# Attention stage of a transformer layer: which probability tiles TensorE takes whole, which engine makes three of the low parts, and in which steps the row maxima are found

## The reference

```python
attn = jnp.einsum('bhqd,bhkd->bhqk', q, k) * SCALE
causal = jnp.tril(jnp.ones((s, s), dtype=bool))
attn = jnp.where(causal[None, None], attn, -jnp.inf)
probs = jax.nn.softmax(attn, axis=-1)
out = jnp.einsum('bhqk,bhkd->bhqd', probs, v)
```

## Time and profile before

| | before |
|---|---|
| median of 3 runs | 1719.4 us (1718.43 to 1723.72) |
| profiled execution: its own time | 1721.68 us |
| profiled execution: span | 1719.9 us |
| PE busy | 1660.3 us (97%) |
| DVE busy | 1161.7 us (68%) |
| ACT busy | 1104.9 us (64%) |
| POOL busy | 906.1 us (53%) |
| mean granted clock of PE | 0.988 |

### The profile page before, as it was taken

One profiled execution on the slowest core, in us unless ns is written; L12 is line 12 of the kernel. 1 busy time (PEld: TensorE's weight loads), 2 busy tenths in 40 slices (PEclk: granted clock), 3 DMA queues, 4 the chain that ended last, 5 costly groups with the idle time before them and its releaser, 6 DMA issues.

```text
span 1719.9 us, 30467 instructions
## 1 busy us (share of the span) xinstructions
PE 1660.3 (97%) x9262; PEld 1369.7 (80%) x9262; DVE 1161.7 (68%) x2377; ACT 1104.9 (64%) x1684; POOL 906.1 (53%) x764
## 2 busy tenths in 40 slices
PE   7999999999999999999986999999999999999996
PEld 7987677767767776776665999999999999999992
DVE  6437777777777777778697676665665566556544
ACT  3222788787878887887686566666665565556544
POOL 2321888878788888882764433434334343343422
PEclk9999999999999999999997999999999999999998
DMA  7676211111111111112664897897987887788776
GB/s 241 188 220 196 62 50 50 49 49 49 49 49 49 49 49 49 49 49 74 232 229 128 287 269 225 245 274 208 281 237 201 224 265 217 208 249 239 192 190 217
DMA packets 103715, 276.87 MB, mean 161 GB/s; under 512 B 19833, under 2 KB 37625, under 8 KB 93625
## 3 DMA queue, kind: packets, MB, share of 16 engines
q1 hardware_dynamic: 78169, 213.29, 38.0%
q0 software_dynamic: 25440, 62.27, 17.4%
HBM read 194.75 MB, written 63.72 MB: 150 GB/s over the span
## 4 chain that ended last, share of the span: by engine, by line
PE 87%; DVE 6%; issue 2%; DMA 2%; ACT 2%; POOL 1%; SPq 0%; DVEq 0%; ACTq 0%; POOLq 0%
PE p_prj L91 26%; PE a_op L883 11%; PE a_mp L842 8%; PE a_sp L901 7%; PE p_at_ps L91 7%; PE p_logit_ps L91 7%; PE e_qp L91 5%; PE a_op L874 5%; PE p_ht_ps L2057 3%; PE e_vp L91 2%; PE p_at_ps L2080 2%; DVE part_max L759 2%; PE a_sp L905 1%; PE a_shared L860 1%; PE a_mp L845 1%
## 5 line engine op out<-in xcount | busy, mean ns | idle before, releaser
L709 POOL TENSOR_TENSOR prob_lo<-prob,prob_hi 128x1024 fp32r<-128x1024 f32 x211 | 451.5, 2157 | 141.6 <-DVE prob_hi L788 132.6
L759 DVE TENSOR_REDUCE part_max<-a_mp 128x1 f32<-128x512 f32 (+2 forms) x600 | 359.5, 610 | 70.5 <-PE a_mp L842 40.4
L1446 POOL DMA_INDIRECT acc_rows<-m_y_out,m_row_ids x108 | 176.1, 1631 | 410.7 <-ACT m_y_out L1615 385.9
L744 ACT ACTIVATE prob<-a_sp 128x1024 f32<-128x1024 f32 x320 | 293.6, 930 | 64.4 <-PE a_sp L905 34.9
L91 PE MATMUL p_prj<-m_w_hi,m_ht_hi 128*128 128x352 f32 x888 | 297.5, 335 | 1.8 <-DVE m_ht_lo L1855 1.4
L91 PE MATMUL p_prj<-m_w_lo,m_ht_hi 128*128 128x352 f32 x888 | 288.0, 324 | 0.0
L91 PE MATMUL p_prj<-m_w_hi,m_ht_lo 128*128 128x352 f32 x888 | 287.0, 323 | 0.0
L1879 DVE TENSOR_TENSOR m_w_lo<-m_w_raw,m_w_hi 128x704 fp32r<-128x704 f32 (+1 forms) x357 | 270.7, 797 | 22.8 <-ACT m_w_hi L1621 22.4
L1621 ACT ACTIVATE m_w_hi<-m_w_raw 128x704 fp32r<-128x704 f32 (+1 forms) x357 | 229.0, 713 | 17.5 <-PE p_prj L91 16.8
L1865 DVE TENSOR_TENSOR m_at_lo<-p_at_ps,m_at_hi 128x384 fp32r<-128x384 f32 x111 | 61.8, 557 | 252.0 <-ACT m_at_hi L1607 252.0
L731 ACT ACTIVATE prob_hi<-prob 128x1024 fp32r<-128x1024 f32 x216 | 203.2, 941 | 6.8
(11 more groups left out here) (314 smaller groups left out, 3336.0 us busy)
## 6 DMA issues: line engine op xcount, KB each, us to landing
m_w_raw<-wexp SPq DMA_DIRECT2D x51, 1408.0 KB
m_w_raw<-wexp SPq DMA_DIRECT2D x51, 768.0 KB
qk_parts<-rows SPq DMA_DIRECT2D x64, 256.0 KB, 3.2
multi<-qk_parts SPq DMA_DIRECT2D x42, 256.0 KB, 5.0
acc_rows<-p_zeros SPq DMA_DIRECT2D x2, 4352.0 KB, 18.8
v_head<-v_all SPq DMA_DIRECT2D x16, 520.0 KB, 3.0
k_stack<-qk_parts SPq DMA_DIRECT2D x21, 256.0 KB, 4.1
q_stack<-qk_parts SPq DMA_DIRECT2D x21, 256.0 KB, 6.2
```

The source lines that it names most:

```text
L709: nc.gpsimd.tensor_tensor(prob_lo[:, t % RING, :, c0:NB], prob[:, t % RING, :, c0:NB], f32(prob_hi[:, t % RING, :, c0:NB]), ALU.subtract). ...
L744: nc.scalar.activation(prob[:, t % RING, :, c0:NB], sp_[:, t % 2, :, c0:NB], ACT.Exp, scale=SCALE).then_inc(prob_ready, 1)
L759: nc.vector.reduce_max(part_max[:, qb, kb:kb + 1], mp[:, n % 2, 0:width], AX_X).then_inc(piece_done, 1)
L1446: nc.gpsimd.indirect_dma_start(acc_dram[sum_of(t)], bass.IndirectOffsetOnAxis(ap=row_id(t), axis=0), y_out[:, t % 4, :], None, compute_op= ...
```

## The change

Four things change, all in the attention:

- In heads 0 to 14 the whole tiles are 10 and 18 in place of 7, 17 and 18. Head 15 keeps 7, 17 and 18; the new function `whole_tiles(h)` chooses.
- `LO_POOL` was all tiles but 0, 1, 10 and the whole ones: 2 to 6, 8, 9, 11 to 16 and 19, 14 tiles. It becomes all but 0, 1, 2 and the whole ones: 3 to 9, 11 to 17 and 19, 15 tiles. DVE makes the low parts of 0, 1 and 2 in place of 0, 1 and 10.
- ACT makes `prob_hi` of tiles 7 and 17 and no longer of 10.
- `PIECES_AT`, the pieces in each step of heads 1 to 14, goes for steps 5 to 19 from 3 4 3 4 2 1 2 1 3 3 3 3 3 3 2 to 3 3 3 3 3 2 3 2 3 3 3 3 2 2 2. The 24th piece then falls in step 13 instead of 14 (as the rule `first_part_done` counts, `row_maxima "a"` moves from step 15 to 14).

```diff
--- before.py
+++ after.py
@@ -529,7 +529,7 @@
 RING = 5
 
 
-PIECES_AT = (0, 0, 0, 0, 0, 3, 4, 3, 4, 2, 1, 2, 1, 3, 3, 3, 3, 3, 3, 2)
+PIECES_AT = (0, 0, 0, 0, 0, 3, 3, 3, 3, 3, 2, 3, 2, 3, 3, 3, 3, 2, 2, 2)
 PIECES_AT_FIRST = (1, 1, 1, 2, 2, 3, 3, 3, 3, 2, 1, 2, 1, 2, 2, 2, 2, 2, 3, 2)
 assert sum(PIECES_AT) == sum(PIECES_AT_FIRST) == NPC and NS == len(PIECES_AT) == len(PIECES_AT_FIRST) and NS % RING == 0
 
@@ -550,9 +550,9 @@
 FW = VW + 1
 
 
-WHOLE = {7, 17, 18}
+WHOLE, WHOLE_LAST = {10, 18}, {7, 17, 18}
 HI_DVE, HI_DVE_LAST = {2, 3, 9}, {1, 2, 3, 4, 5, 8, 9, 11, 13, 15, 19}
-LO_POOL, LO_POOL_LAST = set(range(NS)) - {0, 1, 10} - WHOLE, {0}
+LO_POOL, LO_POOL_LAST = set(range(NS)) - {0, 1, 2} - WHOLE, {0}
 
 def load_projection(sp, flat, wproj_dram, wgate_dram, landed):
 
@@ -566,6 +566,10 @@
 
 def lo_pool_tiles(h):
     return LO_POOL_LAST if isinstance(h, int) and h == H - 1 else LO_POOL
+
+
+def whole_tiles(h):
+    return WHOLE_LAST if isinstance(h, int) and h == H - 1 else WHOLE
 
 
 def count_before(which, t):
@@ -629,7 +633,7 @@
         if t in tiles:
             eng.wait_ge(hi_dve, h * len(HI_DVE) + (count_before(tiles, t) + 1))
         else:
-            eng.wait_ge(hi_act, h * (NS - len(HI_DVE | WHOLE)) + (t - count_before(tiles | WHOLE, t) + 1))
+            eng.wait_ge(hi_act, h * (NS - len(HI_DVE | WHOLE)) + (t - count_before(tiles | whole_tiles(h), t) + 1))
 
     def wait_lo(eng, h, t):
 
@@ -637,7 +641,7 @@
         if t in tiles:
             eng.wait_ge(lo_pool, h * len(LO_POOL) + (count_before(tiles, t) + 1))
         else:
-            eng.wait_ge(lo_dve, h * (NS - len(LO_POOL | WHOLE)) + (t - count_before(tiles | WHOLE, t) + 1))
+            eng.wait_ge(lo_dve, h * (NS - len(LO_POOL | WHOLE)) + (t - count_before(tiles | whole_tiles(h), t) + 1))
 
     def sync_part(sp):
         def load_head(h, p):
@@ -725,7 +729,7 @@
             nc.scalar.activation(o_sb[:, j % 2, :], op[0:VW, :], ACT.Copy).then_inc(out_copied, 1)
 
         def high_part(h, t):
-            if t not in hi_dve_tiles(h) | WHOLE:
+            if t not in hi_dve_tiles(h) | whole_tiles(h):
                 c0 = S_TILES[t][2]
                 act.wait_ge(prob_ready, h * NS + (t + 1))
                 nc.scalar.activation(prob_hi[:, t % RING, :, c0:NB], prob[:, t % RING, :, c0:NB],
@@ -788,7 +792,7 @@
                 nc.vector.tensor_copy(prob_hi[:, t % RING, :, c0:NB], prob[:, t % RING, :, c0:NB]).then_inc(hi_dve, 1)
 
         def low_part(h, t):
-            if t in lo_pool_tiles(h) | WHOLE:
+            if t in lo_pool_tiles(h) | whole_tiles(h):
                 return
             c0 = S_TILES[t][2]
             wait_hi(dve, h, t)
@@ -866,7 +870,7 @@
             j, kp, c0 = S_TILES[t]
             if parts[0] == 0 and t == J_FIRST[j] and not (isinstance(h, int) and h == 0 and j == 0):
                 pe.wait_ge(out_copied, h * NTB + j)
-            if t in WHOLE:
+            if t in whole_tiles(h):
                 if parts[0] == 0:
                     pe.wait_ge(prob_ready, h * NS + (t + 1))
                 for b in parts:
```

## The result

The changed kernel takes 1729.35 us (median of 5 runs, 1728.6 to 1730.3), the kernel before 1720.55 us (5 runs, 1718.43 to 1723.72): ratio 1.0046, 95% interval 1.0034 to 1.0058. The forecast was 1691 us and the range ended at 1707.

The account below looks back on a forecast made before the run. PE was taken as the bound, busy 40.48 of 41.00 us a head. Terms -0.87 - 1.2 + 0.1 = -1.97 us over 14 heads, with heads 0 and 15, gave -28.4: 1719.4 to 1691 us, range 1683 to 1707.

Parts of the forecast that it names:

- PE's own work: Matmuls of whole tiles in steps 1, 11 and 14: two whole tiles lost, one gained, -0.87 us a head.
- The cast of tile 9 under POOL's tiles: DVE's cast now meets a busy POOL: 0.5 us for DVE, 0.1 for PE with late low parts, ends 0 and 1.5.
- Its own sign of being wrong: Wrong if casts of tile 9 take over 1.5 us and PE's pieces wait behind them.
- a rival at 1706 us: POOL or its lock against DVE sets the pace: two locks of 1.0 us reach PE each head; chance 0.20.
- The pieces: PE's waits for DVE's reductions in steps 6, 8 and 15: 1.2 of 1.4 us a head gone with the even table.
- step 15 keeps three, with an output read, and becomes no longer: Step 15's pieces under the even table: step not lengthened, though its 0.25 us late piece was among those counted.
- ACT, POOL and tile 2's low part: ACT's extra high part, POOL's extra full tile and DVE's low part in step 3 all stay hidden: cost 0.
- The loads: Queries for the first piece of step 5 land with 0.0 to 0.9 us to spare: cost 0.
- -1.97: Forecast change a head in us: PE's work -0.87, pieces -1.2, cast and late low parts +0.1.

Follow-up runs that it names:

- e3: The changed kernel with the old table of pieces (new whole tiles, cast of tile 9 on DVE): 1712.65 us, ratio 0.9936 to the kernel before.
- e8: The changed kernel with the cast of tile 9 on ACT and the old table of pieces: 1710.85 us, ratio 0.9936 to the kernel before.
- e1: The changed kernel with only the cast of tile 9 moved from DVE to ACT: 1704.26 us, ratio 0.9893 to the kernel before.
- e6: The changed kernel with 2, 1, 2 pieces in steps 9 to 11 and three in step 12, cast on DVE: 1715.80 us, ratio 0.9967.
- e4: The kernel before with tile 7 alone made ordinary (whole tiles 17 and 18), old table: 1734.68 us, ratio 1.0068.
- e10: The changed kernel with the fitted table of e7, cast of tile 9 on DVE: 1763.33 us, ratio 1.0228 to the kernel before.
- e11: The changed kernel with tiles 7, 17 and 18 whole again; even table and exchanged low parts 2 and 10 kept: 1713.46 us, ratio 0.9956.
- e7: The changed kernel with the cast of tile 9 on ACT and pieces fitted to DVE's other work: 1694.65 us, ratio 0.9842 to the kernel before.
- e2: The kernel before with only the even table of pieces; whole tiles and low part 10 on DVE as before: 1728.88 us, ratio 1.0036.

## Why the prediction was wrong, point by point

**PE's own work, -0.87 us a head: right, if slightly small.** The period is 0.85 shorter in e3 and 0.80 in e8, and both have 0.16 to 0.18 us more in step 5 for late loads inside. What PE saved is then 0.96 to 1.03 (estimate), with small waits for ACT that were not separated.

**The cast of tile 9 under POOL's tiles, +0.1: the step that failed.** I had the mechanism, its rows and a price for DVE, 0 to 1.5 us, and then wrote "I take 0.5 for DVE, with most of it absorbed by steps of two pieces, and 0.1 for PE and late low parts together". Measured: 1.69 us a head (after against e1). Three things were wrong in it. No row stood behind the 0.5: where in POOL's tile the cast would come was never worked out. In heads 2 to 14 it came 1.4 to 1.95 us before the end of tile 8, 1.8 or more in ten of them. The upper end of 1.5 was one row's wait and not a bound; a POOL tile takes 2.4 us, and in e6 DVE waited 2.6. And steps of two pieces do not absorb it: with two pieces in step 10 PE was 1.63 us late in step 11. One piece in step 10 does absorb it: e3 and e4, with casts of 1.6 and 1.9 us and the old table, have no late piece in steps 10 to 12. Its own sign of being wrong, casts of tile 9 over 1.5 us with PE's pieces behind them, is what the profile shows.

The Trainium skill (SBUF — State Buffer, Who interferes with whom) says that whoever issues first gets the shared pair for the whole instruction and the other is fully blocked. The changed kernel agrees: 1.66 us of tile 8 and 0.56 of its own work make the 2.22. In e6 and e10 the cast came 0.02 to 0.38 us before POOL's next tile and still waited for it, so there the order of arrival as the profile shows it did not decide. I had put the skill's reading as a rival at 1706 us and a chance of 0.20, as two blocks of 1.0 us in each head; its place was right, but it was one block that cost PE 1.7, on top of a table worth half of what I had taken.

**The pieces, -1.2: mis-sized, -0.55.** e1 against e8 gives 0.55, and e11 against before, which also exchanges two low parts, 0.56. The late pieces by step say where the rest is. The gaps of steps 6 and 8 did close, 0.65 together. But step 9, with its third piece and its output read, goes from 0.12 to 0.25, and step 15 stays at 0.30: "step 15 keeps three, with an output read, and becomes no longer" should have been read as a wait that stays. The fitted table of e7 moves three pieces, from steps 9, 11 and 15 to steps 10, 12 and 17; steps 9 and 15 fall to 0.02 and 0, and the period to 38.83, 0.64 less than in e1. And the table cannot be judged by itself: with low part 10 on DVE (e2) the same table costs 0.38 us a head, since the old one was thin exactly in the steps where DVE has other work.

**ACT, POOL and tile 2's low part, 0: right as far as the runs tell.** In e1 ACT carries even one high part more than in the change. The only wait of PE for a low part of POOL that the waits view lists from 206 to 790 us is one of 0.5 us. In e11 DVE makes tile 2's low part and POOL tile 10's, and no step is later than in e1.

**The loads, 0: too low.** Head 1 pays 1.0 us and a clock drop, and in heads 5 to 8 and 14 the first piece of step 5 is 0.2 to 0.7 us late; over heads 2 to 14 step 5 goes from 0.05 to 0.17 us a head. With 0.0 us to spare as the lower bound, the cost should have been in the range.

**The clock was not in the sum.** In the changed kernel it fell behind PE's wait in heads 1 and 11 only, while waits of 1.4 to 1.5 us in nine other heads were not followed by it. What made the difference stays open. In e10, with waits of 2.2 to 2.6 us, it fell in every one of heads 2 to 14.

**The sum again with measured terms.** Three runs lead from before to after one step at a time: -0.56 (e11: table and low parts), -0.79 (e1: tiles, with the cast out of the way) and +1.69 (the cast back on DVE) make the +0.34 us a head, where -1.97 was forecast.

**Open.** Who gets its turn when DVE waits and POOL has its next instruction ready. The traces have both outcomes. DVE's cast lost to POOL's next low part in 24 heads of e6 and e10, after waiting 0.02 to 0.38 us. DVE's low part of tile 10 won against POOL's next store in heads 0 to 14 of the kernel before (0.40 to 0.50 us of waiting) and of e4 (1.4 to 1.6 us), and the store then took 1.38. The two groups differ in the length of the wait, in DVE's operation and in POOL's next one, and no run separates these.

## What to carry to other kernels

An engine that looks four fifths busy can owe its good behaviour to where its pauses lie. Filling POOL's pause at tile 7 cost more than the work saved on PE, because a DVE operation that had run in the pause now waited for POOL (the cast in the changed kernel, the low part of tile 10 in e4) and PE had filled both banks before it was done. With one piece in step 10 (e3) PE had not, and the filling gained. Before giving POOL more, look at which DVE operations on two SBUF tiles (or casts from SBUF to SBUF) start inside its new run, price each at the whole rest of a POOL instruction, and count what is queued behind it. And a hand-made uneven table is evidence of something uneven elsewhere: look for what DVE does in the thin steps before evening it out.

## What the runs showed of the hardware that was not expected

- A DVE cast that waits for POOL can lose its turn to POOL's next instruction and wait for that one too: 3.17 us for a cast of 0.68 (e6). In the kernel before and in e4 a DVE subtraction that had waited 0.4 us and more went ahead of POOL's next store.
- After a wait of PE of 2.33 us the granted clock was 0.50 for the next 6 us (e10). After waits of 1.03 us (head 1) and 1.51 us (head 11) of the changed kernel it was 0.57 and 0.60 over 4 us, but after 1.53 us in head 4 of the same execution it stayed at 1.00, and so it did after 1.06 us in head 1 of e7. In this range the length of the wait does not tell.
- A cast of 0.7 us, placed on DVE or on ACT, makes 69 us of difference in the same kernel (e10 against e7): 5.5 us a usual head, of which 2.3 is the wait. Six us at a clock of 0.50 are 3 us of PE's work (estimate), which is most of the rest.
